# Dealing q/k tiles, v tiles, the split and one norm part over the four quarters of a sequence

## The reference, cut to what matters

```python
k, q, v = proj(W_key), proj(W_query), proj(W_value)      # x @ W.T, 16 heads of 16
scores = einsum('bhqd,bhkd->bhqk', q, k) * hd ** -0.5    # causal mask
weight = softmax(scores); out = einsum('bhqk,bhkd->bhqd', weight, v)
x = layernorm(x + out @ W_proj.T * W_proj.shape[-1] ** -0.5)
x = layernorm(x + experts(x))                            # routed: top 129 tokens of each sequence and expert
```

## Time and profile before

| | before |
|---|---|
| median of three runs | 901.45 us (900.26 to 902.26) |
| the profiled execution's own time | 902.58 us |
| its span, first to last instruction | 900.8 us |
| mean granted TensorE clock | 0.962 |
| busy: PE, DVE, ACT, POOL | 820.8, 601.5, 533.2, 473.5 us |
| instructions | 17159 |

### The profile page before, as it was taken

The page is one execution under the profiler, slowest core; times in us unless marked ns, Lnnn a source line. Parts: engine busy times, 40 slices in busy tenths (PEclk is TensorE's granted clock), DMA queues, the critical chain, the costliest instruction groups (busy, mean ns, idle before and its releaser), DMA issues.

```text
span 900.8 us, 17159 instructions
## 1 busy us (share of the span) xinstructions
PE 820.8 (91%) x5876; PEld 613.8 (68%) x5876; DVE 601.5 (67%) x2059; ACT 533.2 (59%) x1048; POOL 473.5 (53%) x642
## 2 busy tenths in 40 slices
PE   4788999999999999998778999999999999999990
PEld 3544454454645454434268999999999999999990
DVE  4488777878788788899858845546464544546464
ACT  2237667667575767676647445555565656555554
POOL 6448565656656565345558356435344435436253
PEclk9669999999999999999789999999999999999995
DMA  4653434536352424520343124335252333523158
GB/s 140 221 182 110 133 110 154 154 106 183 124 151 99 153 90 151 188 72 2 111 174 108 30 43 64 84 83 147 36 130 48 77 95 53 136 31 59 20 146 263
DMA packets 89990, 100.52 MB, mean 112 GB/s; under 512 B 8624, under 2 KB 83376, under 8 KB 89776
## 3 DMA queue, kind: packets, MB, share of 16 engines
q1 hardware_dynamic: 72448, 77.92, 27.0%
q0 software_dynamic: 12800, 16.92, 11.3%
q10 hardware_dynamic: 4656, 4.59, 1.5%
HBM read 65.38 MB, written 33.62 MB: 110 GB/s over the span
## 4 chain that ended last, share of the span: by engine, by line
PE 73%; DVE 13%; ACT 6%; issue 3%; DMA 2%; POOL 1%; ACTq 0%; SPq 0%; POOLq 0%; DVEq 0%
PE y_ps L1357 21%; PE h_ps L1343 19%; PE av_ps L792 7%; PE st_ps L760 5%; DVE n_ps L624 5%; PE n_ps L775 5%; PE stage_ps L809 4%; PE stage_ps L851 3%; PE stage_ps L817 3%; PE tp_ps L1316 2%; ACT pt L522 1%; DVE nmax L624 1%; ACT res L504 1%; PE stage_ps L842 1%; PE stage_ps L801 1%
## 5 line engine op out<-in xcount | busy, mean ns | idle before, releaser
L624 DVE CUSTOM_DVE_ANT_0 n_ps<-n_ps,tri 128x512 f32<-128x512 f32 (+3 forms) x512 | 238.5, 520 | 75.8 <-PE n_ps L775 74.1
L522 ACT ACTIVATE pt<-st_ps 128x512 f32<-128x512 f32 x320 | 184.4, 602 | 64.3 <-PE st_ps L760 49.2
L1357 PE MATMUL y_ps<-w_parts,h_hi 128*128 128x256 f32 (+1 forms) x1152 | 215.2, 281 | 2.1 <-issue 1.5
L1177 ACT ACTIVATE g<-h_ps,b 128x384 f32<-128x384 f32 (+1 forms) x192 | 104.2, 543 | 162.2 <-PE h_ps L1343 134.8
L1357 PEld LDWEIGHTS y_ps<-w_parts,h_hi 128*128 128x128 f32 (+1 forms) x1152 | 172.4, 177 | 6.0 <-issue 1.8
L1149 POOL DMA_INDIRECT acc<-y,tok_no x64 | 102.9, 1608 | 139.8 <-DVE y L1292 129.7
L1343 PE MATMUL h_ps<-tt_hi,w_parts 128*128 128x384 f32 (+1 forms) x768 | 169.7, 323 | 3.6 <-issue 2.0
L1278 DVE TENSOR_TENSOR h_lo<-g,h_hi 128x384 fp32r<-128x384 f32 (+1 forms) x176 | 90.4, 514 | 118.7 <-ACT h_hi L1182 101.4
L451 POOL TENSOR_SCALAR_AFFINE_SELECT pt<-pt 128x256 f32<-128x256 f32 (+1 forms) x320 | 110.6, 363 | 106.8 <-ACT pt L522 106.0
L1357 PE MATMUL y_ps<-w_parts,h_lo 128*128 128x256 f32 (+1 forms) x576 | 161.5, 280 | 0.0
L760 PE MATMUL st_ps<-w_parts 99*128 99x512 bf16 (+3 forms) x512 | 126.4, 309 | 15.7 <-ACT pt L522 14.2
(11 more groups left out here) (192 smaller groups left out, 1079.6 us busy)
## 6 DMA issues: line engine op xcount, KB each, us to landing
w_parts<-part_d SPq DMA_DIRECT2D x192, 128.0 KB, 2.7
w_raw<-in_w SPq DMA_DIRECT2D x16, 1024.0 KB
part_d<-w_raw SPq DMA_DIRECT2D x96, 128.0 KB, 2.1
w_raw<-in_xt SPq DMA_DIRECT2D x8, 512.0 KB, 3.8
res<-in_x SPq DMA_DIRECT2D x8, 512.0 KB, 4.5
x<-res SPq DMA_DIRECT2D x8, 512.0 KB, 3.2
acc<-res SPq DMA_DIRECT2D x8, 512.0 KB, 5.2
fin<-acc SPq DMA_DIRECT2D x4, 512.0 KB, 4.3
```

The source lines that it names most:

```text
L522: nc.scalar.activation(pt[:, slot % PT_RING, n % UP, :], st_ps[at % ST_RING][:, :], ACT.Exp, scale=S_SCALE).then_inc(exp_done, 1)
L624: ins = nc.vector.tensor_tensor_reduce(out=src[:, h, :], in0=src[:, h, :], in1=mask, scale=-1.0, scalar=-BIG_NEG, op0=ALU.add, op1=ALU.min ...
L1177: nc.scalar.activation(g[:, at % G_RING, 0:cols], h_ps[at % H_RING][:, 0:cols], ACT.Gelu, bias=b1[:, e, n:n + 1]).then_inc(g_done, 1)
L1357: ins = nc.tensor.matmul(y_ps[at % Y_RING][0:rows, 0:C], x[:, q % 2, m, toks], w[e % 2][:, m, :], start=i == 0, stop=i == len(terms) - 1)
```

## The change

q/k, v and split of sequences 2 to 7 follow the new entries of STAGES: split of sequence i + 2 at quarter 0, place 2; its q/k tiles at quarter 0, place 9; quarter 1, place 7; quarter 2, place 6; quarter 3, place 0; its v tiles 0 and 1 at quarter 3, places 2 and 9, and 2 and 3 at places 0 and 1 of the next quarter 0 (ahead 1). Sequences 0 and 1 keep the old positions (FIRST_STAGES). Onorm 2 moves from place 8 of quarter 0 to place 0, ahead of the v tile there. No instruction is added or left out.

```diff
 STAGES = (
+    (0, 0, 'onorm', -1, 2),
+    (0, 0, 'v', 1, 2),
+    (0, 1, 'v', 1, 3),
     (0, 1, 'stack', 1, 1),
     (0, 2, 'res', 0, 0),
-    (0, 2, 'qk', 2, 0),
-    (0, 8, 'onorm', -1, 2),
-    (1, 0, 'qk', 2, 1),
+    (0, 2, 'split', 2, 0),
+    (0, 9, 'qk', 2, 0),
+    (1, 7, 'qk', 2, 1),
+    (2, 6, 'qk', 2, 2),
+    (3, 0, 'qk', 2, 3),
+    (3, 2, 'v', 2, 0),
+    (3, 9, 'v', 2, 1),
     (1, 0, 'onorm', -1, 3),
...
-    (1, 7, 'qk', 2, 2),
...
-    (2, 2, 'qk', 2, 3),
...
-    (2, 5, 'v', 2, 0),
-    (2, 6, 'v', 2, 1),
     (2, 7, 'logit', -1, 0),
-    (2, 7, 'v', 2, 2),
-    (2, 8, 'v', 2, 3),
...
     (3, 3, 'onorm', 0, 1),
+)
+
+
+FIRST_STAGES = (
+    (0, 2, 'qk', 2, 0),
+    (1, 0, 'qk', 2, 1),
+    (1, 7, 'qk', 2, 2),
+    (2, 2, 'qk', 2, 3),
+    (2, 5, 'v', 2, 0),
+    (2, 6, 'v', 2, 1),
+    (2, 7, 'v', 2, 2),
+    (2, 8, 'v', 2, 3),
     (3, 5, 'split', 3, 0),
 )
+FIRST = 2
...
                 for gg, kk, stage, ahead, n in STAGES:
-                    if (gg, kk) == (g, k) and 0 <= i + ahead < B and (i, stage, n) not in STARTED:
+                    if (gg, kk) == (g, k) and (FIRST if stage in ("qk", "v", "split") else 0) <= i + ahead < B and (i, stage, n) not in STARTED:
+                        yield stage, i + ahead, n
+                for gg, kk, stage, ahead, n in FIRST_STAGES:
+                    if (gg, kk) == (g, k) and 0 <= i + ahead < FIRST and (i, stage, n) not in STARTED:
                         yield stage, i + ahead, n
                         if (i, stage, n) == (-1, "qk", 1):
                             yield "stack", 1, 0
```

## The result

The changed kernel is slower: 905.79 us (median of 20 runs, 901.37 to 909.55) against 900.71 us for the kernel before (20 runs, 899.36 to 904.19), ratio 1.0053, 95% interval 1.0037 to 1.0068. A second measurement beside the last experiments gave 1.0033 (1.0012 to 1.0054). The forecast was 893.6 us, range 885 to 903.5. Not only the median moved: the runs of the changed kernel spread over 8.2 us, those before over 4.8 us.

A forecast was written before the change was run, and what follows sets the result against it. TensorE was taken as the bound (busy 91%), over a DVE floor. Steady sequences 1 to 4 gave -5.2, sequence 5 -0.8, 6 +0.8, 0 -2.7: -7.9, so 893.6 us from 902.58 less 1.1 us; range 885 to 903.5.

The forecast's parts named there:

- the nm wait of quarter 1: Quarter 1: nm transposes waited for DVE's nmcut behind the q/k tile of place 0; expected gone, quarter booked -1.6 us.
- The split's cover: Quarter 0, place 9: POOL's split half ends near 7.5 us, the q/k tile comes at 9.8; 2 us of cover.
- that of the masks: Place 4 of the next quarter: POOL's masks come some 5 us late, yet 1.4 to 1.5 us remain before AV.
- the preparation: The q/k and v tiles and split of each sequence, said to cost 7.68 us, in quarters 1 and 2.
- The rule: Shared SBUF port pair: a DVE 2-port cast and a GpSimd instruction lock each other out; up to 1.5 us on nmcut.
- Quarter 0 was booked +1.5: Quarter 0: two v tiles 1.68 us, split about 0.4 us on PE, gaps filled, moving onorm free; sum +1.5 us.
- Quarter 2 was booked -2.7: Quarter 2: one q/k and four v tiles leave, one q/k tile comes, -3.36 us, DVE holding back some 0.6; -2.7.
- The clock I had booked only in sequence 0: Sequence 0, quarter 0: moving the q/k tile gives -1.4 us at full clock or +1.5 if low clock lasts; booked +0.5.
- B: Quarter 3: ACT takes PE's place as q/k copies stand ahead of exponentials; +1.2 a sequence, 908.3 us; chance 0.17.
- A: All quarters: work is only carried about, each tile costing PE its full time; sum 0, 901.4 us; chance 0.13.
- C: Quarter 3's idle time takes in nearly all (+0.3), quarter 0 costs +1.0; -3.0 a sequence, 885.2 us; chance 0.12.

The follow-up runs named there:

- the last experiments: Changed kernel with onorm 2 and quarter 2's q/k tile put back, 0.9896; only v, split, first q/k tile moved: onorm back 0.9940, or scores doubled 0.9939.
- early-logits run: The changed kernel with DVE's router logits step at quarter 2, place 5 instead of 7; 899.59 us against 902.00 for the kernel before, ratio 0.9976.
- norm-back run: The changed kernel with onorm 2 back at quarter 0, place 8; 897.46 us against 898.56 for the kernel before, ratio 0.9980.

## Why the prediction was wrong, step by step

What held: quarter 3 waits less for exponentials (3.1 and 1.2 us before, 1.4 and 0.6 us now), the nm wait of quarter 1 is gone, quarter 1 is -1.86 (booked -1.6), and quarter 3 without the lock is +1.33 (booked +1.4). The split's cover held, and that of the masks but for waits of AV of 0.2 us, one in a sequence before and two now. All the sums of the forecast are right as sums. One reading is not: the preparation does not sit in quarters 1 and 2 alone; by PE's count 0.9 us of the 7.68 is in quarter 0 (9.81 us in sequence 4, 8.90 in sequence 6). In sequence 0, whose quarter 2 has no projections, AV waited about 1.1 us for masks behind a q/k tile; I had stepped only through a steady sequence.

**The step that failed** is "DVE's nmcut of place 0 now meets the POOL part of the q/k tile of quarter 2, place 6". The forecast put POOL's part of that tile on nmcut, booked 0.1 us for it, and put nothing on the logits. The rule was right and the instruction was wrong. POOL's three instructions take 3.6 to 3.7 us from place 7 on, and what DVE does in that stretch first is the logits, at place 7. nmcut came when POOL was at its masks, and its casts took 0.17 and 0.18 us in sequence 4. I looked for casts, since the earlier trace rows showed casts, and did not list every DVE instruction beside the moved POOL work. L597 and L599 had two SBUF inputs and stood one place behind. Price in the profile: L614 0.5 us in five sequences, L616 1.0 us in three, 5.5 us in all. By the early-logits run these and what came with them were about 0.8% (1.0053 to 0.9976), and that alone turns the sign.

Two sizes were off, and without any lock they would still have left a steady sequence at -0.49 us (50.38 to 49.89) where -1.3 was booked. Quarter 0 was booked +1.5 and became +1.96, because "Moving onorm inside the quarter is free [...] its bank is free" was false for the tile behind it: onorm's own bank is the next one in turn, 0.50 us a sequence by the norm-back run. With it put back, quarter 0 is +1.45. Quarter 2 was booked -2.7 and became -1.92: with the tile at place 2 it is -2.99. That place 6 stands where PE is dense, while the DVE-paced places 2 to 4 stay empty, is my explanation of it. A tile should be priced by the gap that it leaves as much as by the one that it fills.

The clock I had booked only in sequence 0, as a shift of its first rise. Two falls in mid-attention cost about 2.4 us in this profile (1.6 in sequence 0's AV, 0.8 in sequence 1). How much of the wider spread they make up is not shown. It isn't the locks alone: the early-logits runs, whose profile is free of those on L614 and L616, spread over 7.5 us. And of the 20 runs of the changed kernel the four fastest were granted a mean clock of 0.966 to 0.969, the four slowest 0.958 to 0.964.

As for the rivals, B had the sign, and 908.3 us for 905.8, but by ACT's copies in quarter 3; there it had +3.2 us where +1.33 was found without the lock, and the early-logits run leaves ACT as it was and is faster than before, so B's cause is refuted and its nearness is luck. A's sum of nothing is what sequences 2 and 3 come to, but not by its terms (+2.6 in quarter 3, +2.25 in quarter 0). C's +0.3 in quarter 3 is out by the same +1.33. The sum over sequences 0 to 6, from first to last score tile: booked -7.9, profiled +4.3 (340.25 to 344.57 us).

## What to carry to other kernels

When work of one engine is moved, list what every other engine does in the stretch where it lands, and above all DVE instructions with two SBUF inputs beside POOL instructions that read SBUF: a 0.2 us instruction then lasted as long as POOL's. Even quarters are no aim in themselves; put a tile where its engine waits for another anyway, and check which bank in the ring its neighbour will need. Where a change makes the times spread, compare sequences with equal work within one profile: they show waits that come in some sequences only, and clock falls, both of which a median hides. And before a fall of the clock is put down to a quiet stretch, look at the same stretch where the clock did not fall.

## What the runs showed of the hardware that was not expected

The granted clock fell to 0.50 in the midst of a loop in which PE is busy 96% of the time (47.39 of 49.37 us), after a stretch of 3.4 us with 2.25 us busy, at a price of 1.6 us each; and it stayed at 1.00 after the same stretch in the sequences before (2.23 and 2.26 us busy). Score matmuls done twice there cost nothing (49.37 us a sequence with and without them at full clock), and in the one profile with them no fall came. And the lock is a matter of nanoseconds: where DVE's instruction started 5 to 7 ns after POOL's it took 1.20 us, and at 1 to 5 ns 0.19 us, with POOL's at 1.15 and at 1.21 us.
